# First attention of a two-layer transformer block: the turning back, division and storing of each group of four heads placed one pair later in the common order of the engines

## The reference

```
def _L0_attn_ref(x, Wqkv, bqkv, Wproj, bproj):        # H = 16 heads, DH = 16
    qkv = x @ Wqkv.T + bqkv
    qkv = qkv.reshape(b, t, H, 3 * DH).transpose(0, 2, 1, 3)
    q, k, v = jnp.split(qkv, 3, axis=-1)
    q = q * rope + _rotate(q) * (1.0 - rope)
    k = k * rope + _rotate(k) * (1.0 - rope)
    att = jnp.einsum('bhtd,bhsd->bhts', q, k) * (1.0 / math.sqrt(DH))
    att = jnp.where(causal, att, -jnp.inf)
    att = jax.nn.softmax(att, axis=-1)
    y = jnp.einsum('bhts,bhsd->bhtd', att, v)
    y = y.transpose(0, 2, 1, 3).reshape(b, t, d)
    return y @ Wproj.T + bproj
x = x + _L0_attn_ref(_layernorm(x, axis=-1), ...)
```

## Time and profile before

| | us |
|---|---|
| median of 3 runs | 2893.51 |
| lowest and highest run | 2885.59, 2895.51 |
| the profiled execution, its own time | 2884.65 |
| span of the profiled execution | 2883.0 |
| TensorE busy (share of the span) | 2443.0 (85%) |
| VectorE | 1826.3 (63%) |
| ScalarE | 1345.0 (47%) |
| GpSimd | 815.3 (28%) |

### The profile page before, as it was taken

The page is one execution under the profiler, slowest core; times in us unless marked ns, Lnnn a source line. Parts: engine busy times, 40 slices in busy tenths (PEclk is TensorE's granted clock), DMA queues, the critical chain, the costliest instruction groups (busy, mean ns, idle before and its releaser), DMA issues. The chain is left out here.

```text
span 2883.0 us, 54564 instructions
## 1 busy us (share of the span) xinstructions
PE 2443.0 (85%) x20412; PEld 2178.7 (76%) x20412; DVE 1826.3 (63%) x3236; ACT 1345.0 (47%) x2053; POOL 815.3 (28%) x1194
## 2 busy tenths in 40 slices
PE   4888888884199999935677888869999999999999
PEld 3555656653199999933566667759999999999999
DVE  7555555547288888849888887727554544544544
ACT  1455545541177777733333344334544545445454
POOL 6454554504500000044566665530000000000000
PEclk8799999986599999967799989989999999999999
DMA  9993000001467777746555555424322222322222
GB/s 307 323 334 118 1 2 1 1 1 48 141 220 233 239 234 230 231 141 148 139 127 134 138 128 136 122 76 159 110 90 86 86 90 86 90 89 91 83 78 88
DMA packets 194351, 373.36 MB, mean 130 GB/s; under 512 B 28708, under 2 KB 104680, under 8 KB 193128
## 3 DMA queue, kind: packets, MB, share of 16 engines
q1 hardware_dynamic: 184792, 343.31, 39.4%
q0 software_dynamic: 9360, 27.27, 2.8%
HBM read 336.95 MB, written 100.66 MB: 152 GB/s over the span
## 5 line engine op out<-in xcount | busy, mean ns | idle before, releaser
L2325 DVE TENSOR_TENSOR e_h_lo<-e_h,e_h_hi 128x512 fp32r<-128x512 f32 x320 | 222.2, 694 | 300.7 <-ACT e_h_hi L2401 300.7
L2463 PE MATMUL e_h_ps<-e_yT_hi,e_w_hi 128*128 128x256 f32 x1280 | 362.3, 283 | 3.1 <-ACT e_h L2387 2.4
L2479 PE MATMUL e_y_ps<-e_w_hi,e_h_hi 128*128 128x256 f32 x1280 | 358.8, 280 | 2.4 <-DVE e_h_lo L2325 2.2
L2463 PE MATMUL e_h_ps<-e_yT_lo,e_w_hi 128*128 128x256 f32 x1280 | 358.2, 280 | 0.0
L2463 PE MATMUL e_h_ps<-e_yT_hi,e_w_lo 128*128 128x256 f32 x1280 | 358.1, 280 | 0.0
L2479 PE MATMUL e_y_ps<-e_w_hi,e_h_lo 128*128 128x256 f32 x1280 | 355.4, 278 | 0.0
L2479 PE MATMUL e_y_ps<-e_w_lo,e_h_hi 128*128 128x256 f32 x1280 | 355.3, 278 | 0.0
L2401 ACT ACTIVATE e_h_hi<-e_h 128x512 fp32r<-128x512 f32 x320 | 202.2, 632 | 277.5 <-DVE e_h L2320 221.0
L2387 ACT ACTIVATE e_h<-e_h_ps,e_b 128x512 f32<-128x512 f32 x320 | 218.8, 684 | 174.5 <-PE e_h_ps L2463 152.2
L2320 DVE TENSOR_TENSOR e_h<-e_h,e_spread 128x512 f32<-128x512 f32 x256 | 176.9, 691 | 133.2 <-ACT e_h L2387 132.1
L468 DVE TENSOR_REDUCE a_top<-a_ring 128x2 f32<-128x1024 f32 (+3 forms) x256 | 202.8, 819 | 70.6 <-PE a_ring L676 70.5
(11 more groups left out here) (364 smaller groups left out, 6845.1 us busy)
## 6 DMA issues: line engine op xcount, KB each, us to landing
e_w<-in_w SPq DMA_DIRECT2D x78, 1024.0 KB, 5.9
e_spread<-share_store SPq DMA_DIRECT2D x512, 128.0 KB, 2.9
a_keys<-rows_store SPq DMA_DIRECT2D x128, 256.0 KB, 4.9
a_queries<-rows_store SPq DMA_DIRECT2D x86, 256.0 KB, 5.2
a_running_hidden<-rows_store SPq DMA_DIRECT2D x42, 256.0 KB, 4.9
e_xs<-sorted_x SPq DMA_DIRECT2D x39, 256.0 KB, 5.4
sorted_y<-e_ys POOLq DMA_DIRECT2D x39, 256.0 KB, 5.9
e_stage_buf<-in_w_all SPq DMA_DIRECT2D x10, 512.0 KB, 3.7
```

Source lines behind the costliest of these rows:

```text
L2325: dve.tensor_tensor(h_parts[q % 2][1][:, :], h[:, q % 2, :], h_parts[q % 2][0][:, :], ALU.subtract).then_inc(h_lo.sem, h_lo.tick())
L2463: last = pe.matmul(h_ps[q % 2][:, cols], l, r, start=(m == 0), stop=(m == len(ops) - 1))
L2479: last = pe.matmul(y_ps[n][:, 0:D], h_parts[q % 2][a][:, n * P:(n + 1) * P], w2[b][:, c, :], start=(q == 0 and m == 0), stop=(q == CH - 1 ...
```

## The change

The unit o is taken from the end of the step, where it had the offset -1, and put behind b1 with the offset -2. The unrolling runs one step further, so that the o of r = 7 still has a step (step 9, which holds nothing else). All of `ORDER`, `PLACE` and `TURNED` follow from the list. No instruction's text is changed.

```
-        STEP = (("qk", 3), ("a0", 2), ("b0", 0), ("v0", -1), ("m", 1), ("a1", 2), ("b1", 0), ("v1", -1), ("a2", 2),
-                ("v2", -1), ("b2", 0), ("v3", -1), ("h", -1), ("o", -1))
+        STEP = (("qk", 3), ("a0", 2), ("b0", 0), ("v0", -1), ("m", 1), ("a1", 2), ("b1", 0), ("o", -2), ("v1", -1), ("a2", 2),
+                ("v2", -1), ("b2", 0), ("v3", -1), ("h", -1))
...
-        for step in range(-3, PAIRS + 1):
+        for step in range(-3, PAIRS + 2):
```

## The result

| | us |
|---|---|
| before, median of 4 runs (lowest, highest) | 2891.52 (2885.59, 2895.51) |
| after, median of 4 runs (lowest, highest) | 2860.02 (2855.59, 2865.62) |
| ratio of the times, with its 95% interval | 0.9894 [0.9868, 0.9919] |
| the profiled execution of before, its own time | 2884.65 |
| the profiled execution of after, its own time | 2865.62 |

The change makes the kernel 1.1% faster, 31.5 us between the medians. 2866 was forecast, 27.6 us won. The two profiled executions are only 19.0 us apart, since that of before was faster than each of the four timed ones and that of after is the slowest of its four. So where the time went is read from intervals inside a sequence, not from the two ends.

What follows compares the result with a forecast made beforehand. TensorE's order of work was taken to set the pace. Six middle sequences (21.8 us), sequence 7 (3.9) and sequence 0 (1.9) sum to 27.6 us won, from the median of 2893.51 to 2866 us; range 2855 to 2881.

Steps and rivals of the forecast that it cites:

- What bounds: First attention: TensorE's order sets the pace; L712 waits 32 times for ScalarE's copy, 26.5 us; at most 24 waits go.
- Two of its signs: Signs expected in the profile after: a middle sequence 3.6 us shorter, and a0(6) waiting some 0.2 for a maximum.
- What goes: Wait and transposes freed at the old place: 1.23 us in step 3, 1.42 in step 5, 1.3 in step 7.
- The cover in steps 3 and 5: Transposes cost 0.59 behind b1, perhaps 0.1 more; b2's waits of 0.54 and 0.55 cover them, leaving 0.1 uncovered each.
- The loss in step 3: 0.71 us of VectorE division before a2's maximum makes a0(6) some 0.2 late; with 0.1 uncovered transposes, 0.22 is subtracted.
- Sequence 0: First sequence, VectorE busier with statistics: 0.6 won in step 3, next to nothing in step 5, 1.3 in step 7; 1.9 together.
- The new wait for L528: In step 3, L712 shares pT with m(4) and so waits for ScalarE's copy: on the edge, zero to 0.05 us.
- The sum: 3.63 us per sequence 1 to 6 (21.8), 3.9 in sequence 7, 1.9 in sequence 0: 27.6; upper bound 31.6.
- A: Steps 3 and 5 give back their gain, as L712 pushes a2, b2 and the ring: 2884.5 us; chance 0.12.
- B: Slower: VectorE becomes the bound of steps 3 and 5, 44 us lost against 31.6 won: 2906 us; chance 0.04.
- C: The clock: cold tails of sequences vanish, 4 us more won (2862), or all eight turn cold, 7 lost (2873); chance 0.08.
- D: Nothing is won, because another limit paces a sequence: 2893.5 us; chance 0.03.

Runs made afterwards that it cites:

- c_before: The kernel before, unedited, run and profiled a second time: 2879.76 us, 0.9989 of before.
- e_double: The kernel after, with the four transposes of each o done twice with the same result: 2866.84 us, 0.9934 of before.
- e_maxfirst: The kernel after, with VectorE taking a2's maximum ahead of the reciprocal and multiply of o, TensorE's order unchanged: 2855.56 us, 0.9898 of before.
- e_early: The kernel after, with o between a0 and b0 of the next step instead of behind b1: 2906.35 us, 1.0069 of before.
- e_r13: The kernel before, with o moved for groups 0 and 1 (r = 1, 3) only: 2871.64 us, 0.9955 of before.
- e_afterqk: The kernel after, with o between qk and a0 of the next step instead of behind b1: 2878.77 us, 0.9980 of before.
- c_after: The kernel after, unedited, run and profiled a second time: 2855.17 us, 0.9890 of before.
- e_r5: The kernel before, with o moved for group 2 (r = 5) only: 2878.27 us, 0.9968 of before.
- e_next: The kernel after, with group 3's o also moved, behind qk(0) of the next sequence: 2837.86 us, 0.9855 of before.

## Why the prediction was right, point by point

**What bounds.** TensorE's order, with its 32 waits for the copy: right. 24 waits went with the place of the unit and 8 stayed, and each stretch became shorter by what its wait and transposes had taken. 26.5 us fell to 6.2 (forecast about 7). Two of its signs came out otherwise: a middle sequence is 4.2 us shorter, not 3.6, and a0(6) waits for no maximum, where 0.2 was expected.

**What goes.** 1.23, 1.42 and 1.3 were forecast as freed, 1.30, 1.50 and 1.38 were won net. So the losses together were nothing, and the freed time was a little more than taken. In step 3, before, qk(6) started 1.06 behind the start of the copy h(1) (245.96 to 247.02); after, it starts 0.25 ahead of it (243.32, 243.07). That is 1.31 freed. The 0.08 over 1.23 come mostly from v3(1): its recorded end is 242.72 + 0.42 = 243.14, and qk(6) starts 0.07 before that, so the next unit does not wait for the recorded end, as the prediction took it. In step 7 the exps start 0.11 before the recorded end of the copy (264.08 + 0.59 = 264.67, 264.56), which makes 1.28 + 0.11 = 1.39 out of 1.3.

**The cover in steps 3 and 5, mis-sized: 0.10 taken, 0 measured.** The transposes cost TensorE 0.70 in step 3: from b1(3)'s last row (246.40) to a2(5) (247.17) it is 0.77, where it had been 0.07. That is the 0.59 of the prediction and the 0.1 that it allowed for the change from half-height tiles to full ones and back. The cover, too, was larger than the 0.54 of b2's wait: from the start of a2(5) to that of a0(6) it is 250.42 to 252.65 before, 2.23, and 247.17 to 248.70 after, 1.53, again 0.70. So the loss is 0. The list of waits agrees: b2's wait for maxima, 8.6 us in 16 waits in c_before, became 0.9 in one. The other four transposes of e_double add 0.41 to 0.43, less than 0.70; they follow transposes of the same shape.

**The loss in step 3, mis-sized: 0.22 taken, 0 measured.** From qk(6) to a0(6) it is 5.63 us in both kernels (247.02 to 252.65, 243.07 to 248.70), so a0(6) came exactly when due. The prediction had a2's maximum done at 252.7, 5.68 behind qk(6), and a0(6) 0.17 later. Measured, the maximum ended 5.57 behind qk(6) (248.64) and a0(6) started 0.06 after that: 0.11 less for the maximum, since from the end of a1's maxima (246.13 + 1.29 = 247.42) it is 1.22 where 0.71 + 0.57 = 1.28 had been taken and the rest is rounding, and 0.11 less for the latency. e_maxfirst took the division out of the way and won nothing in these sequences, which shows that the term is 0. It is a narrow zero, with nothing to spare beyond the latency.

**Sequence 0.** VectorE has the statistics there too, and a loss in step 3 exists: 0.6 (e_maxfirst), against 0.7 forecast. The prediction put the gain from h(3) to h(5) at next to nothing, because a0(7) would have to wait for the maximum of a2(6). That reading was wrong: a0(7) stands two places behind a2(6) in the ring of three tiles, and in the kernel after it starts without idle time, before that maximum. What waits for it is b0(5), one unit later, and 0.50 us are won. The timeline of the kernel after, sequence 0:

```profile
111.63 0.51 PE L671 MATMUL a_ring<-a_kq_T 64*128 64x512 f32 x2
...
112.34 0.69 DVE L468 TENSOR_REDUCE a_top<-a_ring 128x2 f32<-128x512 f32 x1
...
113.09 0.50 PE L685 MATMUL a_ring<-a_qT_max,a_kq_T 64*128 64x512 f32 x2 [0.85 <-DVE a_top L468]
```

**The new wait for L528.** On the edge, as said, and it fell on the good side by 0.14 us. The rule of the Trainium skill that was weighed here (VectorE: DVE Perf Modes, "The DRAIN you can't avoid") would have added 0.16 behind the multiply. The prediction set it aside by the reciprocal, which can't test it: the reciprocal takes 0.26 us, and the rule's 266 ns leave nothing to drain. The kernel after does test it: the multiply runs from 247.62 to 248.04 and the maximum behind it starts at 247.96, so this trace doesn't show that drain.

**The sum.** 3.63 per middle sequence was forecast, 4.18 came; 27.6 in all against 32.2 by the intervals, which is even above the 31.6 that the prediction gave as its upper bound for the order; the bound left out the 0.08 and the 0.11 of overlap named above. The times won 31.5 and, on another chip, 31.3.

**The rivals.** A (the gain given back in steps 3 and 5) and D (nothing) are refuted by the intervals. B, VectorE as the bound of steps 3 and 5, didn't occur here. A kindred wait, which B had not priced, occurs in e_early: m waits 11.3 us for the multiply L487 when the unit stands ahead of b0, about as much as L712's wait for the copy fell (26.5 to 15.5). Behind b1 the next m follows much later, and it never arises.

**C, the clock.** The cold tails went, as one half of C said: counted over the profiles, 11 of 40 sequences with group 2 in its old place or uncovered had one (before, c_before, e_r13, e_early, e_afterqk), and 0 of 48 with it behind b1 (after, c_after, e_double, e_r5, e_maxfirst, e_next; in one of these the copy came 0.6 late, at a granted clock of 1.00). With 1.06 us idle before v0(7), or 0.69 in e_double, the tail kept the full clock each time, with 1.70 not always. But the borders took more time too, which C had not named: 7 us on average, from 296.0 to 303.5 in the four profiles of after, c_after, e_r5 and e_maxfirst against 291.2 to 295.5 in before, c_before, e_afterqk and e_r13. e_early, with 309.0 and cold tails as well, fits neither group (the borders of e_double and e_next hold other work), so this split is an observation on few profiles and no cause. That the times won nearly what the order alone gives (31.5 and 32.2) is in part chance: the clock's two effects, each of several us in single profiles, nearly cancel. Why the borders lose clock stays open, since no run changed that alone.

## What to carry to other kernels

A unit that waits for another engine's copy is moved behind work that covers the copy, and then its new neighbours in each shared buffer and queue are checked, not only its own wait: the same kernel was 1.1% faster with the unit behind b1, 0.2% with it behind qk, and 0.7% slower with it ahead of b0 (there most of the loss went with the clock). Idle time that lies beside a moved piece of work is real cover (4 transposes cost 0, 8 cost 0.4), but it is spent once. To see what a piece of work costs and what covers it, one measures from the last row before it and to the next row behind it, in both kernels, and not by the idle times alone (0.70 against 0.70 here, where the idle time read 0.54). Where gains are read in a trace, intervals between two marks of the same loop body at equal granted clock are sharper than the whole span, whose two profiles here differed by 19 us for a gain of 31.

## What the runs showed of the hardware

The same border of a sequence took 41.7 or 46.7 us within one execution of the kernel after, at a granted clock of 1.00 and 0.85, and the time at half clock in one phase went from 20.6 us (c_before) to 105.6 (e_early) while the order of work changed little. Over the 17 runs of the kernel before on one chip the time falls, on the whole, with the mean clock, from 2893.4 us at 0.923 to 2874.9 at 0.933.

Behind the last mask matmul of a b unit (L690, on 64 rows) the next matmul on 64 rows starts 0.07 us later (250.35, 250.42), the transposes on 128 rows 0.19 later (246.40, 246.59). Behind the first of four transposes the next unit starts after 0.41 us if it works on 128 rows (246.61, 247.02) and after 0.58 if on 64 (246.59, 247.17). So changing the tile height, both ways together, took some 0.3 us here (estimate, from these four).

The Trainium skill (TensorE: Matmul & The Clock Gate, "A second HAM failure mode: psum-queue depth-cycling") says of another kernel that frequent short idle spells between groups of matmuls made the clock swing between its two levels. The runs bear out part at most: L712, m behind L487 and b2 wait 55 times in e_early, which loses most clock, against 48 in c_before. But in the kernel after they wait 9 times, and it has no less half clock (49.1 and 44.5 us against 38.7 and 20.6), so the rule doesn't order these kernels.
